# First layer of a two-layer attention kernel: both mixes behind the scores, two turns a row in a score bank, source cast on ScalarE

## What is computed

```python
# layer 0: x = x + L0(_gn(x)); every row m attends over its own 256 tokens
x = _layernorm(x1d, norm_w, norm_b)
qkv = (x @ qkv_w.T).reshape(*x.shape[:-1], c, 3 * h)        # 8 heads of 32
aff = jnp.einsum('bmich,bmjch->bmijh', q, k)
gate = jax.nn.sigmoid(x @ gate_w.T + gate_b)
bias = x2d @ x2d_w.T * factor
weights = jax.nn.softmax(aff + bias[:, None], axis=-2)
out = jnp.einsum('bmrch,bmirh->bmich', v, weights) * gate
out = out.reshape(*x.shape[:-1], c * h) @ final_w.T + final_b
# layer 1: x = x + L1(_gn(x)); 4 heads of 64, only keys within 16 of the query
```

## Times and profile before

| | us |
|---|---|
| median of 3 executions | 3706.16 (3704.67 to 3711.67) |
| the profiled execution | 3711.91 |
| its span | 3710.0 |
| up to about 212 us | weights, statistics of x, pair bias, first group norm |
| about 212 to 2397 us | first layer |
| about 2397 to 3710 us | second group norm and second layer |

### The profile page before, as it was taken

The page is one execution under the profiler, slowest core; times in us unless marked ns, Lnnn a source line. Parts: engine busy times, 40 slices in busy tenths (PEclk is TensorE's granted clock), DMA queues, the critical chain, the costliest instruction groups (busy, mean ns, idle before and its releaser), DMA issues.

```text
span 3710.0 us, 122532 instructions
## 1 busy us (share of the span) xinstructions
PE 3428.1 (92%) x36747; PEld 2986.1 (80%) x36747; DVE 3129.4 (84%) x11359; ACT 2693.5 (73%) x8871; POOL 1993.3 (54%) x3723
## 2 busy tenths in 40 slices
PE   4469999999999999999999999799999999999998
PEld 1157878777878787878787787599999999999998
DVE  4479999999999999999999999778888888888887
ACT  1148888888888888888888888567677667766776
POOL 0046767666666666666666666434434344444443
PEclk8579999999999999999999999899999999999999
DMA  9921111111111111111111111111111111111111
GB/s 360 354 71 46 49 46 48 48 45 50 43 51 42 51 42 51 42 51 42 51 42 51 42 51 42 41 41 51 51 56 51 51 51 57 51 51 52 55 51 47
DMA packets 189032, 238.42 MB, mean 64 GB/s; under 512 B 11824, under 2 KB 176176, under 8 KB 184752
## 3 DMA queue, kind: packets, MB, share of 16 engines
q1 hardware_dynamic: 184368, 204.17, 17.4%
q10 hardware_dynamic: 4608, 33.56, 2.5%
HBM read 170.57 MB, written 67.11 MB: 64 GB/s over the span
## 4 chain that ended last, share of the span: by engine, by line
PE 49%; DVE 16%; issue 13%; POOL 11%; ACT 5%; DMA 4%; DVEq 1%; ACTq 0%; POOLq 0%; SPq 0%
PE work L464 20%; POOL prob L359 6%; PE score L597 5%; PE work L473 5%; PE turn L504 5%; PE mix L630 4%; ACT prob L702 4%; PE score L491 3%; DMA x_chunk<-xT 3%; PE turn L614 3%; POOL g_tok L373 2%; POOL g_tok L370 2%; DVE kT L954 2%; DVE att L939 2%; DVE y_sb L890 2%
## 5 line engine op out<-in xcount | busy, mean ns | idle before, releaser
L359 POOL TENSOR_SCALAR prob<-prob,row_inv 128x256 f32<-128x256 f32 x2048 | 1049.0, 530 | 683.3 <-DVE row_inv L908 670.7
L464 PE MATMUL work<-src,w 128*128 128x256 f32 x7680 | 1074.1, 289 | 36.4 <-DVE y_sb L890 29.9
L702 ACT ACTIVATE prob<-prob,row_min 128x256 f32<-128x256 f32 x2048 | 1022.6, 504 | 39.2 <-DVE row_min L902 39.2
L464 PEld LDWEIGHTS work<-src,w 128*128 128x128 f32 x7680 | 951.9, 189 | 118.9 <-DVE y_sb L890 59.7
L902 DVE CUSTOM_DVE_ANT_0 prob<-score,neg_bias 128x256 f32<-128x256 f32 x2048 | 753.1, 419 | 111.7 <-PE score L491 100.9
L402 POOL TENSOR_SCALAR prob<-prob,row_inv 128x160 f32<-128x160 f32 x1024 | 387.9, 397 | 765.0 <-DVE row_inv L1012 765.0
L504 PE MATMUL turn<-ident,prob 128*128 128x128 f32 x4096 | 627.9, 276 | 35.2 <-DVE probT L913 29.7
L708 ACT COPY probT<-turn 128x512 f32<-128x512 f32 x512 | 299.5, 585 | 351.4 <-PE turn L504 351.4
L765 ACT ACTIVATE prob<-prob,row_min 128x160 f32<-128x160 f32 x1024 | 431.1, 426 | 136.4 <-DVE row_min L1005 136.3
L504 PEld LDWEIGHTS turn<-ident,prob 128*128 128x128 f32 x4096 | 463.9, 141 | 78.8 <-POOL prob L359 47.0
L464 PE MATMUL work<-att,wf 128*128 128x256 f32 x3072 | 429.3, 289 | 3.6 <-DVE att L939 2.2
(11 more groups left out here) (99 smaller groups left out, 5528.2 us busy)
## 6 DMA issues: line engine op xcount, KB each, us to landing
pair_chunk<-pairT ACTq DMA_DIRECT2D x32, 1024.0 KB, 7.7
x_chunk<-xT SPq DMA_DIRECT2D x32, 1024.0 KB, 8.4
x_sb<-xT SPq DMA_DIRECT2D x128, 256.0 KB, 3.4
x_tok<-x_nat SPq DMA_DIRECT2D x128, 256.0 KB, 3.3
x1T<-y_sb SPq DMA_DIRECT2D x128, 256.0 KB, 2.2
x_sb<-x1T SPq DMA_DIRECT2D x128, 256.0 KB, 2.9
outT<-y_sb SPq DMA_DIRECT2D x128, 256.0 KB, 2.2
prob<-w_d SPq DMA_DIRECT2D x1, 1024.0 KB, 8.2
```

The costliest lines, as they stand in the source:

```text
L359: pool.tensor_scalar(prob[:, h, ib], prob[:, h, ib], row_inv[:, h, ib:ib + 1], 1.0, ALU.mult, ALU.mult).then_inc(norm_done[0], 1)
L464: ins = pe.matmul(out[:, cb], w[:, of_w, kb, cols + cb * P:cols + (cb + 1) * P], x[:, of_x, kb], start=n == 0, stop=n == len(terms) - 1)
L702: act.activation(prob[:, h, ib], prob[:, h, ib], ACT.Exp, bias=row_min[:, h, ib:ib + 1], scale=-1.0, accum_out=row_sum[:, h, ib:ib + 1]).t ...
```

## The change

Only the first layer's order and a few of its instructions change; the second layer gets another bias vector.

TensorE: the pass now runs queries, scores of heads 4 to 7, both mixes of the last row, turn 0, transposes of `xn`, turn 1, keys, turns 2 and 3, values, scores 0 to 3 of the next row, turn 4, gate, turn 5, y of the last row, turns 6 and 7. Turns 3 and 7 go to `score[:, 0]`. Queries, keys and gate use `work[:, 0]`, the transposes, values and y use `work[:, 1]`.

ScalarE casts `xnT` to the high half of `src`, behind a wait for its own `xnT`. VectorE: y of row m-2 (instead of m-1) is one addition without the bias, its statistics are taken once for two rows, the layer norm's statistics are taken one pass earlier (row m+3, `ahead`), `xn` stands between the minima of heads 5 and 6. The missing bias is put into the second group norm's mean and into `y_bias`, which the second layer adds. GpSimd's multiply and add are one row further ahead with the scaling of heads 4 and 5 between them. SP writes y one pass later and loads `x_tok` one row further ahead, behind GpSimd's multiply (`gn_scaled`).

```diff
@@ gpsimd, body0
+                if far.exists:
+                    wait(pool, ln_var_done, far.times(1, 1))
+                    pool.tensor_tensor(ln_rstd[:], ln_var[:], minus_half[:], ALU.pow).then_inc(ln_rstd_done, 1)
                 if m.exists:
                     norms(m, 1)
+                if ahead.exists:
+                    wait(pool, x_tok_in[ahead.base % 2], ahead.times(16, 16, of=2))
+                    wait(pool, xn_done, nxt.times(TB, TB))
+                    pool.tensor_tensor(g, x_tok[:, ahead.base % 2], ...).then_inc(gn_scaled, 1)
+                if m.exists:
+                    norms(m, 2)
+                if ahead.exists:
+                    pool.tensor_tensor(g, g, ..., ALU.add).then_inc(g_done[0], 1)
                 if m.exists:
                     norms(m, 3)
                 if nxt.exists:
                     norms(nxt, 0)
@@ tensor, scores and turns
                     wait(pe, min_done[0], r.times(TB * H0, TB * HPG * hg))
+                    wait(pe, turn_done[0][1], r.times(PAIRS0, 2 * hg - 2))
...
+                    if h % HPG == HPG - 1:
+                        to = score[:, 0].rearrange("p b t -> p (b t)")
@@ scalar, body0 after the change
+                if nxt.exists:  q_ps -> nqT high
+                if m.exists:
+                    exps(m, 3)
+                    exps(m, 4)
+                    turn_copy(0)
+                if far.exists:
+                    wait(act, t2_done, far.times(1, 1))
+                    for cb in range(CB):
+                        act.activation(xnT[:, cb], work[:, 1, cb], ACT.Identity, ...).then_inc(xnT_done, 1)
+                    wait(act, xnT_done, far.times(CB, CB))
+                    wait(act, gate_ps, far.times(1, -1))
+                    act.copy(src[:, far.base % 2, HIGH], xnT[:]).then_inc(src_high[0], 1)
+                exps(m, 5);  k_ps -> kT high;  turn_copy(2);  att_sum -> att high;  exps(m, 6)
+                v_ps -> v_sb;  exps(m, 7);  turn_copy(4);  exps(nxt, 0);  gate tanh;  exps(nxt, 1)
+                turn_copy(6);  exps(nxt, 2)
@@ vector, body0 after the change
+                y of row m-2:  dve.tensor_tensor(y_sb[...], work[:, 1], x_sb[...], ALU.add)
+                nqT low of nxt;  mins(m, 4);  inverse(m, 1);  mins(m, 5)
+                xn of far;  mins(m, 6);  mins(m, 7);  att_sum of last
+                turn_copy(1);  inverse(m, 2);  kT low of nxt;  turn_copy(3);  src low of far;  att low of last
+                mins(nxt, 0);  inverse(m, 3);  mins(nxt, 1);  mins(nxt, 2);  turn_copy(5)
+                mins(nxt, 3);  inverse(nxt, 0);  bn_stats of ahead;  turn_copy(7);  bn_aggr and ln_var of ahead
+                if done.exists and done.base % 2 == 1:  bn_stats of y of two rows, 512 wide
```

More of the change, by code:

```diff
@@ L544, in body0 @@
                     turns(4)
+                if nxt.exists:
+                    wait(pe, k_done[0], nxt.times(1, 1))
+                    project(work[:, 0], w0, 3 * CH, x).then_inc(gate_ps, 1)
+                if m.exists:
+                    turns(5)
                 if last.exists:
@@ L547, in body0 @@
                     if nxt.exists:
[L548 to L550 removed]
+                        wait(pe, v_done[0], nxt.times(1, 1))
                     else:
[L552 removed]
+                        wait(pe, y_done[0], m.times(1, -1))
                     project(work[:, 1], wf0, 0, att).then_inc(y_ps[0], 1)
                 if m.exists:
[L555 to L574 removed]
+                    turns(6)
                     turns(7)
@@ L747, in body0 @@
                 if nxt.exists:
-                    exps(nxt, 3)
-                    wait(act, gate_ps, nxt.times(1, 1))
-                    wait(act, att_sum_done, nxt.times(1, -1))
-                    for hg in range(HG):
-                        act.activation(gate[:, nxt.base % 2, hg], work[:, 1, hg], ACT.Tanh, scale=0.5,
-                                       bias=half_gate_b[:, hg:hg + 1]).then_inc(gate_done, 1)
+                    exps(nxt, 2)
             over_rows(act, 2, 1, body0)
@@ L880, in split @@
                                   ).then_inc(src_done[n], 1)
-            def residual(n, last, bank, bias):
-                wait(dve, y_ps[n], last.times(1, 1))
-                wait(dve, y_out[n][last.base % 2], last.times(16, 0, of=2))
-                if n == 0:
-                    wait(dve, x_in[n][last.base % XSLOTS], last.times(16, 16, of=XSLOTS))
-                    apart(dve, dve_passed)
-                for ob in range(CB):
-                    dve.scalar_tensor_tensor(out=y_sb[:, last.base % 2, ob], in0=work[:, bank, ob], scalar=bias[:, ob:ob + 1],
-                                             in1=x_sb[:, last.base % XSLOTS, ob], op0=ALU.add, op1=ALU.add
-                                             ).then_inc(y_done[n], 1)
             def body0(m):
-                last, nxt, far = m + -1, m + 1, m + 2
+                last, nxt, far, ahead = m + -1, m + 1, m + 2, m + 3
                 def mins(r, h):
@@ L940, in body0 @@
                                       ).then_inc(att_done[0], 1)
-                if far.exists:
-                    wait(dve, g_done[0], far.times(1, 1))
+                if nxt.exists:
+                    mins(nxt, 0)
+                if m.exists:
+                    inverse(m, 3)
+                if nxt.exists:
+                    mins(nxt, 1)
+                    mins(nxt, 2)
+                if m.exists:
+                    turn_copy(5, turn[:])
+                if nxt.exists:
+                    mins(nxt, 3)
@@ L983, in body0 @@
-                if far.exists:
-                    wait(dve, xnT_done, far.times(CB, CB))
-                    wait(dve, gate_ps, far.times(1, -1))
-                    split(0, far, xnT[:])
-                if m.exists:
-                    turn_copy(7)
-            over_rows(dve, 2, 1, body0)
-            dve.wait_ge(y_stats, CB * ROWS)
+                if done.exists and done.base % 2 == 1:
+                    wait(dve, y_done[0], done.times(1, 1))
+                    apart(dve, dve_passed)
+                    for ob in range(CB):
+                        pair = done.base // 2
+                        at = slice(pair, pair + 1) if done.loop is None else bass.ds(done.times(1, 0, of=2), 1)
+                        dve.bn_stats(gstat1[:, ob, at], y_sb[:, ob].rearrange("p r t -> p (r t)")).then_inc(y_stats, 1)
@@ L1026, in body1 @@
                 if (last + -1).exists:
-                    residual(1, last + -1, 1, vec1_sb[:, 2])
+                    done = last + -1
+                    wait(dve, y_ps[1], done.times(1, 1))
+                    wait(dve, y_out[1][done.base % 2], done.times(16, 0, of=2))
+                    for ob in range(CB):
+                        dve.scalar_tensor_tensor(out=y_sb[:, ob, done.base % 2], in0=work[:, 1, ob],
+                                                 scalar=y_bias[:, ob:ob + 1], in1=x_sb[:, done.base % XSLOTS, ob],
+                                                 op0=ALU.add, op1=ALU.add).then_inc(y_done[1], 1)
                 if m.exists:
```

285 lines of the change are left out of this document (148 added, 137 removed).

## The result

| | us |
|---|---|
| before, median of 4 executions | 3708.9 (3704.67 to 3711.67) |
| with the change, median of 4 | 3742.53 (3739.55 to 3747.49) |
| ratio | 1.0093, 95% interval 1.0076 to 1.0110 |
| the profiled execution's span | 3737.7 (before: 3710.0) |

The change makes the kernel 0.9% slower, clear of the interval. The prediction said 3698 and "faster" as the likeliest sign (0.42); 3742.5 lies in its range (3655 to 3775), but the time moved the other way.

A forecast was written before the change was run, and what follows sets the result against it. Engine order, not one engine's work, bounds the first layer: the ring's 16.60 us plus 0.1 and 0.05 makes 16.75 a row instead of 16.81, -8 us over 127 rows, the ends -0.6; forecast 3698 us, range 3655 to 3775.

The forecast's parts named there:

- the ring: First layer's row: closed chain from xn over TensorE, ScalarE's queue and VectorE's queue back to xn, 16.60 us; chance 0.55.
- VectorE's arc: VectorE's stretch of the ring, from the inverse of the next row's first heads to xn: 5.95 us.
- The first rival: VectorE's work alone sets the row, which shrinks by the 0.65 us removed: 3623 us; chance 0.15.
- ScalarE's arc: ScalarE's stretch of the ring, from xnT until the next row's exp 1 can be read: 9.77 us.
- the hand-over: From VectorE's end of xn to TensorE's start 0.15 us, from there to ScalarE 0.73 us.
- The wait for the queries: In rows without y statistics VectorE arrives 0.62 us early and is held at the queries: 0.2 us every second row.
- (2): The inverse of the next row's first heads, on VectorE: 0.09 us to the next start.
- (3): xn on VectorE: 0.73 us, plus 0.05 (0 to 0.3) for running beside GpSimd's normalisations.
- (1): y's sum on VectorE waits for the statistics of the row pair before, claimed done a row ago; no term given.
- Rival 2: GpSimd's shift addition meets VectorE's attention low half: 1.3 us enter, 0.7 covered; row 17.2 to 17.3, 3756 us; chance 0.20.
- Rival 3: Lags of 0.1 us in three more hand-overs between engines: row 17.0 us, 3730 us; chance 0.10.
- the ends: First layer's start and the group norm between the layers: -0.6 us in sum, between -4 and +3.

The follow-up runs named there:

- the pair of spare statistics: The changed kernel with one more unread 512-wide VectorE statistic a row: behind turn copy 1 3739.1 us, behind turn copy 7 3847.7 us.
- filler: The changed kernel with 16 identity transposes on TensorE ahead of its wait for xn, in rows where it is 2 us: 3724.8 us, ratio 1.0049.

## Why the prediction was right and wrong

**Right: the ring.** It decides, it has the arcs that the prediction gave it, and most signs it named were there: ScalarE without a gap behind xnT, VectorE waiting before the inverse and for the keys (0.4 us where 0.7 was named). The mechanism was right; the terms of VectorE's arc and the clock were not. ScalarE's idle 2 us came in two parts, 0.7 in front of xnT and 1.1 in front of the exponentials of head 4, on average; the second part was the sign of the second ring, on which the experiment with `xn` ahead ran aground. 0.6 us of VectorE's work a row cost nothing outside it and 108.6 us inside. The first rival, VectorE's work alone (3623), fell with it. By the rule of the Trainium skill ("Perfetto Trace Analysis", Identifying the Most-Contended Engine), to optimise the engine with the highest occupancy first, that rival was the forecast; the pair of spare statistics speaks against it here. ScalarE's arc was forecast at 9.77 and measured at 9.81, its work a row at 14.45 and 14.46, VectorE's at 14.79 and 15.10, 0.31 more.

**Right by luck: short rows.** For rows without y statistics the terms give 16.60 - 0.62 + 0.2 + 0.05 = 16.23; measured 16.16 to 16.25. But the parts don't fit. Over the 45 such rows at full clock between 300 and 2300 us ScalarE's arc is 9.84, VectorE's from the inverse to the end of `xn` 5.61, and the hand-over 0.75. The terms were 9.77, 5.95 - 0.62 = 5.33, and 0.88. The wait for the queries, for which the 0.2 stood, is not there at all (0.00), and its room was taken by the same two mis-sized steps, (2) and (3), that long rows have.

**Wrong: long rows.** For these the terms give 16.60 + 0.62 + 0.05 = 17.27; measured 17.60 to 17.72. Three terms of VectorE's arc were mis-sized. (1) y's wait: the prediction read "waits for statistics of the row pair before, on VectorE itself, done a row ago". They are made by the instruction just in front, because y reuses the buffer that they read, and cost 0.26 in the row shown, 0.21 on average over 44 long rows at full clock. (2) From the start of the inverse to the next start 0.30, not the 0.09 of the earlier trace rows: there the inverse had not been waited for. It is 0.30 in all 103 rows of the kernel after, between 300 and 2300 us, in which this inverse had waited for ScalarE, and 0.17 to 0.18 in the 14 in which it had not; where minima follow an inverse, 0.20 and 0.09. Why the next one starts later behind a waiting instruction I can't say; nothing here takes it apart. (3) xn 0.82 beside GpSimd instead of 0.73, of which the forecast had taken 0.05. Together 0.26 + 0.21 + 0.09 = 0.56. Less that 0.05, less 0.12 in the hand-over to ScalarE (0.76, forecast 0.88) and with 0.04 on ScalarE's arc this is 0.43, and 17.27 becomes 17.70. At full clock the row is 16.876 (filler), 0.13 above the forecast: 16 us.

**Missed: TensorE's clock.** The prediction said that TensorE waits anyway and took its speed as given, since the trace of before showed the full clock in the rows. It didn't ask what a wait of 2 us in one place does to it, and so put this term at nothing without a reason. The filler shows the price with all that follows: 0.131 a row, 16.6 us, as much as all mis-sized terms together. The two make up the miss of the rows, 16.0 + 16.6 = 32.6 us between the -8 that was forecast and +24.5.

**Rival 2** (the meeting) had 0.20 and 3756. In the kernel after it happens in 14 of 127 rows, each behind a low clock, 9 times to the attention low half and 5 times to the source's; in the other rows VectorE comes first, as the prediction had it by a tenth: the addition mostly starts 0.23 us after the attention low half has ended. The prediction read one meeting in the trace of before; there is a second one, an attention low half of 0.93 us at 2326.45 us. And by its own terms its row is 16.75 + 0.6 = 17.35, 3774 us, not 17.2 to 17.3 and 3756. **Rival 3** (small lags, 17.0 a row, 3730) had only 0.10 and came nearest in the row, though not by the lags that it named.

**The sign.** The rows were forecast at -8 and came at +24.5; the ends at -0.6 and came at -2.9 + 4.5 - 3.3 = -1.7. Of these the start of the layer is the mis-sized one, 4.5 where 1.0 was written for one more stage, and the end of the layer came at -3.3 where its terms give -3.5 + 1.0 + 0.6 + 0.3 = -1.6. The -2.9 ahead of them is no gain of the change, since that point lies anywhere between 208.5 and 217.5 us in the experiments, which have the same code up to there. The second layer, "left at its time", is 4.9 longer with the same instructions but one vector. Between the first and last instruction of its GpSimd norm it has 1268.0 us before, 1274.1 after, and between 1270.7 and 1275.6 in the experiments, which don't touch it. What sets that stays open.

## What to carry to other kernels

When work is tight on all engines, look for the ring: the chain through the queues that comes back to its own start one row later. Its sum is the row, and a step's price is decided by whether it stands in it. Here moving the same statistics from one place of VectorE's order to another was worth 84 us, of which some 17 are the clock's by the filler's price. After every shortening look for the next ring, and look at what an engine does while it waits: here TensorE's wait for `xn` was free in the sum, but its clock was found lower behind it in one row of four, and that was not free.

## What was not expected of the hardware

- TensorE's granted clock fell to 1.2 GHz for 3.4 us at a time in a kernel in which TensorE is busy 92% of the stage. Between 300 and 2300 us of the kernel after it fell 14 times, in one of four rows in which TensorE had stood about 2 us for `xn`, and with GpSimd's addition held 18 times. Where that wait was at most 1.5 us (statistics in each row) or 1.7 (cast on VectorE), or was filled, it did not fall there. With `xn` ahead of the minima it fell 12 times, behind two waits of 0.2 to 0.4 and 1.3 us with the transposes between them. With the addition held each time cost about 0.8 us of the row.
- VectorE's subtraction of two SBUF operands beside GpSimd's addition took 1.6 to 1.9 us instead of 0.68, in 58 meetings in two kernels. If VectorE was first by more than 0.04 us it lost little or nothing, and GpSimd's instruction took longer: the addition 1.71 to 1.79 us instead of 1.29, four scalings beside the low halves 2.84 instead of 1.85. In five meetings VectorE started 0.02 to 0.04 us first by the profile and lost all the same. This agrees with the Trainium skill ("SBUF — State Buffer", Who interferes with whom). The kernel with 0.44 us more on VectorE ahead of the attention low half has 44 meetings, the kernel after 14.
